# Output and down projections of a fused attention and feed-forward kernel: exact float32 products replaced by three float32r products each

## What is computed

```
h = shift_token(x);  q, k, v = h @ wqkv           # 8 heads of 64, l2norm and rotary on q, k
o = local_attention(q, k, v)                      # windows of 128, each query sees its own and the previous window
x = x + o @ wo                                    # "output product", 512 -> 256
h = layernorm(shift_token(x)) * ln_g + ln_b
a, g = split(h @ w1 + b1)                         # 2 x 682 columns
x = x + (a * gelu(g)) @ w2 + b2                   # "down product", 682 -> 256
```

## Time and profile before

| what | value |
|---|---|
| median of three runs | 1547.39 us |
| the profiled execution, its own time | 1549.65 us |
| span of that execution in the trace | 1547.9 us |
| TensorE (PE) busy | 1471.8 us, 95% |
| DVE, ACT, POOL busy | 895.6, 791.1, 637.7 us |
| mean granted clock of TensorE | 0.98 |
| PE's share of the chain that ended last | 79% |

### The profile page before, as it was taken

One profiled execution on the slowest core, in us unless ns is written; L12 is line 12 of the kernel. 1 busy time (PEld: TensorE's weight loads), 2 busy tenths in 40 slices (PEclk: granted clock), 3 DMA queues, 4 the chain that ended last, 5 costly groups with the idle time before them and its releaser, 6 DMA issues.

```text
span 1547.9 us, 23333 instructions
## 1 busy us (share of the span) xinstructions
PE 1471.8 (95%) x7572; PEld 1020.7 (66%) x7572; DVE 895.6 (58%) x2555; ACT 791.1 (51%) x2073; POOL 637.7 (41%) x424
## 2 busy tenths in 40 slices
PE   3999988999999999999999999999999999999977
PEld 2777766676767676767575766666666666666745
DVE  3677647565656565656565655565655555555635
ACT  1555545464646454645455554646464636464642
POOL 2343326353526253535353534444453535353510
PEclk7999989999999999999999989999999999999998
DMA  6110110000000000000001010000000000000045
GB/s 188 41 54 27 41 64 1 1 1 1 0 0 0 0 0 0 0 0 0 0 1 55 1 55 1 1 0 0 0 0 0 0 0 0 0 0 0 0 141 185
DMA packets 35239, 33.28 MB, mean 21 GB/s; under 512 B 8364, under 2 KB 32896, under 8 KB 35200
## 3 DMA queue, kind: packets, MB, share of 16 engines
q1 hardware_dynamic: 35200, 32.79, 6.6%
HBM read 24.39 MB, written 8.39 MB: 21 GB/s over the span
## 4 chain that ended last, share of the span: by engine, by line
PE 79%; ACT 3%; issue 1%; POOL 1%; DVE 1%; ACTq 0%; POOLq 0%
PE l_psF L1159 9%; PE l_ring L1129 8%; PE l_psP L1129 8%; PE l_psF L1244 7%; PE l_ring L1159 7%; PE l_ring L1227 7%; PE l_ring L1168 6%; PE l_psP L1211 6%; PE l_psS L1168 5%; PE l_psF L1197 4%; PE l_psS L1180 3%; PE l_psS L1197 2%; ACT l_att L875 2%; PE l_psF L1143 2%; PE l_psF L1137 2%
## 5 line engine op out<-in xcount | busy, mean ns | idle before, releaser
L758 POOL TENSOR_TENSOR l_att<-l_att 128x1024 f32<-128x1024 f32 x64 | 153.5, 2398 | 353.5 <-DVE l_att L967 353.5
L796 POOL TENSOR_TENSOR l_att<-l_att,l_rinv 128x1024 f32<-128x1024 f32 x64 | 121.3, 1895 | 84.9 <-DVE l_rinv L1019 84.9
L857 ACT ACTIVATE l_att<-l_psP 128x384 f32<-128x384 f32 (+1 forms) x128 | 70.4, 550 | 164.4 <-PE l_psP L1211 164.4
L1024 DVE COPY l_att<-l_psP 128x384 f32<-128x384 f32 (+1 forms) x128 | 78.8, 615 | 122.1 <-PE l_psP L1211 121.7
L1211 PEld LDWEIGHTS l_psP<-ident,l_att 128*128 128x128 f32 x896 | 100.2, 142 | 50.2 <-issue 45.9
L800 POOL TENSOR_TENSOR l_att<-l_att,l_rinv 128x256 f32<-128x256 f32 x64 | 39.3, 614 | 210.8 <-DVE l_rinv L1019 210.8
L1211 PE MATMUL l_psP<-ident,l_att 128*128 128x128 f32 x896 | 123.8, 279 | 2.1 <-DVE l_att L1024 2.1
L765 POOL TENSOR_TENSOR l_att<-l_att,l_rn 128x1024 f32<-128x1024 f32 x64 | 121.4, 1908 | 0.0
L1244 PE MATMUL l_psF<-l_att,w_wo 128*128 128x512 f32 x256 | 118.5, 606 | 0.0
L875 ACT ACTIVATE l_att<-l_psF,l_nb 128x256 f32<-128x256 f32 x256 | 117.8, 482 | 0.1
L1227 PE MATMUL l_ring<-l_att 128*64 128x256 f32 (+1 forms) x1024 | 111.0, 358 | 4.4 <-issue 2.9
(11 more groups left out here) (171 smaller groups left out, 3695.2 us busy)
## 6 DMA issues: line engine op xcount, KB each, us to landing
a_tables<-in_x SPq DMA_DIRECT2D x8, 512.0 KB, 4.1
scratch_s<-a_o SPq DMA_DIRECT2D x8, 512.0 KB, 3.0
l_att<-in_x SPq DMA_DIRECT2D x8, 512.0 KB, 8.6
l_att<-scratch_s SPq DMA_DIRECT2D x8, 512.0 KB, 9.0
out_dram<-l_att SPq DMA_DIRECT2D x7, 512.0 KB, 7.6
aw_stage<-in_wqkv SPq DMA_DIRECT2D x2, 768.0 KB, 7.3
l_att<-in_wqkv SPq DMA_DIRECT2D x2, 768.0 KB, 5.2
w_w<-in_w SPq DMA_DIRECT2D x2, 640.0 KB
```

What stands on the lines that cost most here:

```text
L758: pool.tensor_tensor(rot[:, t, :], rot[:, t, :], t2[t % 2], ALU.add).then_inc(S["added"], 1)
L796: pool.tensor_tensor(pr, pr, along(inv, 2 * P), ALU.mult).then_inc(S["p_done"], 1)
```

## The change

It touches six things.

1. `output` and `down` use three float32r products for each float32 product: (w_hi, data_hi), (w_hi, data_lo), (w_lo, data_hi). The weights wo and w2 are split once for each layer: high parts on ACT, low parts on DVE.
2. The gated tiles: gelu writes into a gate buffer, DVE's `gated` multiplies in place, ACT's new `u_high` rounds it to U_hi, and DVE's new `u_low` makes U_lo. In merged steps the gate buffers are the four halves of two of the probability buffers (`between_units`), and softmax(0) and softmax(1) wait for the low parts that still read them.
3. The attention result: `o_evac` writes OT_hi, and DVE's new `o_low` makes OT_lo.
4. `mean` and `variance` are one float32 product each: DVE adds the two halves of h (into rstdF), and the two halves of the squares (`sum_squares`), beforehand.
5. The order: down's half c = 0 runs as four tiles before unit 2, then one tile each in units 2 and 4; half c = 1 as tiles 0 to 2, 3 to 4 and 5 in units 7, 8 and 9. add_ffn(0) moves from unit 4 to unit 5. less_mean moves into rotate(0), and ACT's square stands before the second tile's squares.
6. Memory: several buffers share places, and the staging place of wqkv moves. The scratch size for DMA descriptors is set to 4096.

```diff
+    def high_wo(self, act, layer):
+        act.wait_ge(self.S["wo_in"], 16 * (layer + 1))
+        act.activation(self.wo_hi[:, :, :], self.wo_raw[:, :, :], ACT.Copy).then_inc(self.S["wo_hi"], 1)
+
+    def low_wo(self, dve, layer):
+        dve.wait_ge(self.S["wo_hi"], layer + 1)
+        dve.tensor_tensor(self.wo_lo[:, :, :], self.wo_raw[:, :, :], self.wo_hi[:, :, :].bitcast(F32), ALU.subtract).then_inc(self.S["wo_lo"], 1)
...
+    def high_w2(self, act, layer):
+        act.wait_ge(self.S["w2_in"], 32 * (layer + 1))
+        for r, k in self.w2_parts(layer):
+            last = act.activation(self.w2_hi[r, k, :], self.w2_raw[r, k, :], ACT.Copy)
+        last.then_inc(self.S["w2_hi"], 1)
+
+    def low_w2(self, dve, layer):
+        dve.wait_ge(self.S["w2_hi"], layer + 1)
+        for r, k in self.w2_parts(layer):
+            last = dve.tensor_tensor(self.w2_lo[r, k, :], self.w2_raw[r, k, :], self.w2_hi[r, k, :].bitcast(F32), ALU.subtract)
...
                         W.high_w1(act, 0, stage1, k)
+                    W.high_wo(act, 0)
+                    W.high_w2(act, 0)
...
+                    W.low_wo(dve, 0)
+                    W.low_w2(dve, 0)
...
-                if j >= 2:
-                    ge(act, S["u_done"], HT * u + j - 1)
+                if j >= 4:
+                    ge(act, S["u_lo"], HT * u + j - 3)
...
+            def u_high(i, j, attn):
+                rows = P if j < HFULL else HREM
+                ge(act, S["u_done"], HT * (i - 1) + j + 1)
+                act.activation(U_hi[0:rows, j, :], gate_of(j, attn)[0:rows, :], ACT.Copy).then_inc(S["u_hi"], 1)
...
-                act.activation(OT[:, pair, :], ring[pair % 2][:, :], ACT.Copy).then_inc(S["o_sb"], 1)
-
-            def softmax(i, u):
+                act.activation(OT_hi[:, pair, :], ring[pair % 2][:, :], ACT.Copy).then_inc(S["o_hi"], 1)
+
+            def softmax(i, u, ffn):
                 ge(act, S["pT_ps"], UNITS * i + u - 2)
+                if ffn and u < 2:
+                    ge(act, S["u_lo"], HT * (i - 1) + 2 * u + 4)
...
                 if attn:
                     evacuate(i, 0)
-                    evacuate(i, 1, square if ffn else None)
+                    if ffn:
+                        square()
+                    evacuate(i, 1)
...
                 for j in range(HT):
                     if ffn:
-                        gelu(i, j, lf)
+                        gelu(i, j, lf, attn)
+                    if ffn and j:
+                        u_high(i, j - 1, attn)
                     if attn and j < TT:
                         q_evac(i, j)
                     if attn and j == 1:
                         high((i + 1) % B, i + 2)
+                    if turn and j == TT:
+                        W.high_wo(act, 1)
                 if attn:
                     act.preload_act_table_set(NLE)
+                    if ffn:
+                        u_high(i, HT - 1, attn)
...
+                    if turn:
+                        W.high_w2(act, 1)
...
+            def u_low(i, j, attn):
+                rows = P if j < HFULL else HREM
+                ge(dve, S["u_hi"], HT * (i - 1) + j + 1)
+                dve.tensor_tensor(U_lo[0:rows, j, :], gate_of(j, attn)[0:rows, :], U_hi[0:rows, j, :].bitcast(F32), ALU.subtract).then_inc(S["u_lo"], 1)
...
+            def o_low(i, pair):
+                ge(dve, S["o_hi"], PAIRS * i + pair + 1)
+                dve.tensor_tensor(OT_lo[:, pair, :], ring[pair % 2][:, :], OT_hi[:, pair, :].bitcast(F32), ALU.subtract).then_inc(S["o_lo"], 1)
...
+                def sum_squares():
+                    ge(dve, S["sqF_done"], i)
+                    dve.tensor_tensor(sqF[:, 0, :], sqF[:, 0, :], sqF[:, 1, :], ALU.add).then_inc(S["sq_sum"], 1)
...
                 if attn:
-                    rotate(i, 0, la)
+                    rotate(i, 0, la, less_mean if ffn else None)
                 if attn and ffn:
-                    less_mean()
+                    sum_squares()
...
                     combine(2)
                     combine(3)
-                    gated(i, 0, lf)
+                    gated(i, 0, lf, attn)
                     combine(4)
...
                 for j in range(HT):
                     if ffn:
-                        gated(i, j, lf)
+                        gated(i, j, lf, attn)
                     if attn and j < TT:
                         k_evac(i, j)
+                    if ffn and j:
+                        u_low(i, j - 1, attn)
+                if ffn:
+                    u_low(i, HT - 1, attn)
                 if turn:
 
                     ge(dve, S["u_done"], HT * i)
                     dve.memset(stage1[:, :, 2 * HFULL * P:], 0.0).then_inc(WS["w1pad"], 1)
+                    W.low_wo(dve, 1)
                 if attn:
                     for u in range(UNITS + 3):
                         if u < UNITS:
                             least_of(i, u)
                         if 1 <= u <= UNITS:
                             inverse_sum(i, u - 1)
-                        if u == 4 and ffn:
+                        if u == 5 and ffn:
                             add_ffn(i, 0, lf)
                         if u >= 3:
                             p_evac(i, u - 3)
+                        if u in (7, 9):
+                            o_low(i, (u - 7) // 2)
                         if turn and UNITS <= u < UNITS + KD:
                             W.low_w1(dve, 1, stage1, u - UNITS)
+                if attn:
+                    o_low(i, PAIRS - 2)
                 if ffn:
                     add_ffn(i, 1, lf)
+                if attn:
+                    o_low(i, PAIRS - 1)
                 if last:
                     for k in range(KD):
                         W.low_wqkv(dve, 1, stage, k)
+                if turn:
+                    W.low_w2(dve, 1)
                 if attn:
                     ge(dve, S["wo_ps"], i + 1)
                     for k in range(KD):
...
                     ge(dve, S["x_attn"], KD * (i + 1))
-                    dve.tensor_scalar(dF, h_view(xT, i - B * la), 1.0, None, ALU.mult).then_inc(S["h_ready"], 1)
+                    h = h_view(xT, i - B * la)
+                    dve.tensor_tensor(rstdF[:, :].unsqueeze(1), h[:, 0:1, :], h[:, 1:2, :], ALU.add).then_inc(S["h_sum"], 1)
+                    dve.tensor_scalar(dF, h, 1.0, None, ALU.mult).then_inc(S["h_ready"], 1)
...
             def mean(i):
-                ge(pe, S["h_ready"], i)
-                for k in range(KD):
-                    last = pe.matmul(psF[:, 0:N], ones[:, :], dF[:, k], start=(k == 0), stop=(k == KD - 1))
-                last.then_inc(S["mean_ps"], 1)
+                ge(pe, S["h_sum"], i)
+                pe.matmul(psF[:, 0:N], ones[:, :], rstdF[:, :], start=True, stop=True).then_inc(S["mean_ps"], 1)
...
             def variance(i):
-                ge(pe, S["sqF_done"], i)
-                for k in range(KD):
-                    last = pe.matmul(psF[:, N:2 * N], ones[:, :], sqF[:, k, :], start=(k == 0), stop=(k == KD - 1))
-                last.then_inc(S["var_ps"], 1)
+                ge(pe, S["sq_sum"], i)
+                pe.matmul(psF[:, N:2 * N], ones[:, :], sqF[:, 0, :], start=True, stop=True).then_inc(S["var_ps"], 1)
...
-                    if c == 0 and k >= HFULL - 1:
-                        ge(pe, S["u_done"], HT * (i - 1) + k + 1)
-                    last = pe.matmul(down_of[c], w2[:, k, c * P:(c + 1) * P], U[:, k, :], start=(k == 0), stop=(k == HT - 1))
+                    if c == 0:
+                        ge(pe, S["u_lo"], HT * (i - 1) + k + 1)
+                    for m, (w, u) in enumerate(((W.w2_hi, U_hi), (W.w2_hi, U_lo), (W.w2_lo, U_hi))):
+                        last = pe.matmul(down_of[c], w[:, k, c * P:(c + 1) * P], u[:, k, :], start=(k == 0 and m == 0), stop=(k == HT - 1 and m == 2))
...
-                    ge(pe, S["o_sb"], PAIRS * i + pair - 1)
+                    ge(pe, S["o_lo"], PAIRS * i + pair - 1)
...
-                    ge(pe, S["o_sb"], PAIRS * i + a + 1)
+                    ge(pe, S["o_lo"], PAIRS * i + a + 1)
                     for c in range(KD):
-                        last = pe.matmul(psF[:, c * N:(c + 1) * N], wo[:, a, c * P:(c + 1) * P], OT[:, a, :],
-                                         start=(a == 0), stop=(a == PAIRS - 1))
+                        for m, (w, o) in enumerate(((W.wo_hi, OT_hi), (W.wo_hi, OT_lo), (W.wo_lo, OT_hi))):
+                            last = pe.matmul(psF[:, c * N:(c + 1) * N], w[:, a, c * P:(c + 1) * P], o[:, a, :],
+                                             start=(a == 0 and m == 0), stop=(a == PAIRS - 1 and m == 2))
...
-                    down(i, 0, range(0, 3))
+                    down(i, 0, range(0, 4))
                 if attn:
                     for u in range(2, UNITS + 3):
                         if u < UNITS:
                             scores(i, u)
-                        if ffn and 2 <= u <= 4:
```

(11 more changed lines are left out.)

109 lines of the change are left out of this document (67 added, 42 removed).

## The result

The changed kernel takes 1523.69 us (median of 4 runs, 1522.57 to 1525.51), against 1547.97 (4 runs) for the kernel before: a ratio of 0.984, 95% interval [0.983, 0.986]. It is 24 us faster where 45 were forecast, and the time lies 3.7 us above the range of 1480 to 1520. The profiled execution took 1522.57 us, its span 1520.8. In experiments 5 and 6 one execution of four took 1984 and 1982 us at a mean granted clock of 0.65, so their medians here are of the other three.

The account below looks back on a forecast made before the run. PE (TensorE) was taken as the bound, busy 78.50 of 79.24 us in a merged step. Fifteen steps at 3.3 us less (49.5) and +4.9 for single places gave -44.6 us: 1502.8 us against the median, range 1480 to 1520.

Parts of the forecast that it names:

- rival 3: Merged steps: clock falls at the scores(2) hole, some 4 us or more a step, 1563 us in all; chance 0.04.
- Front of a step: Projections to transposes(1): PE 1.7 us earlier, a new wait of 0.6 us at transposes(1), gain 1.1 us a step.
- Middle: hidden(5) to scores(7): least_of(0) 2.3 us late, PE stands 1.7 us at scores(2); net 0.4 us lost a step.
- End of a step: After scores(7): down's second half 1.0 us and output 1.5 us shorter, no new wait; gain 2.6 us a step.
- (a): Before the layers block: low parts of wo and w2 enter DVE's queue, +1.4 us.
- (b): Step 0, attention only: only output gets shorter, -1.5 us.
- (c): Step 7: low_wqkv is queued behind o_low(3) and step 8's projections wait for it, +1.5 us.
- (d): Step 8, the turn: high_wo and low_wo stand before least_of(0), +2.2 us, less 0.6 for output(0) at half clock.
- (e): Step 16: sum_squares stands behind combine(1), which waits for a DMA; after what down gives back, +1.9 us.
- Rival 1: Merged steps: PE's saving arrives nearly whole, 4.3 to 5.5 us a step, 1488 down to 1470 us; chance 0.17.
- Rival 2: Front: POOL holds DVE's sum_squares, gain falls to 1.4 us a step, 1531 us; chance 0.14 with other long waits.
- Rival 4: The float32r products gain nothing, as alternating weights run slower; 1547 + 8 us or so; chance 0.02.

Follow-up runs that it names:

- experiment 5: Changed kernel with one move on DVE: the sixth low part, u_low(5), stands behind least_of(0) instead of ahead of it; 1489.34 us, ratio 0.962.
- exp. 6: Against experiment 5: u_high(5) moved behind softmax(0) on ACT, u_low(5) behind least_of(1) and the first reciprocal on DVE; 1519.04 us, ratio 0.982.
- exp. 1: Changed kernel with 7 unneeded float32r products in each merged step, in PE's standstill before scores(2); 1510.22 us, ratio 0.976.
- exp. 2: Changed kernel with 3 unneeded float32r products in each merged step, in PE's standstill before scores(2); 1511.05 us, ratio 0.976.
- experiment 4: Kernel before the change with two unused 128x1024 multiplications on DVE ahead of least_of(0) in merged steps but the turn; 1582.83 us, ratio 1.022.
- exp. 3: Changed kernel with one unused 128x1024 multiplication on DVE ahead of least_of(0) in merged steps but the turn; 1554.9 us, ratio 1.005.
- Experiment 9: On experiment 5: sum_squares ahead of combine(1) in step 16, one low part of the next projection weights ahead of step 7's last o_low; 1483.59 us.
- experiment 8: On experiment 5: mean and variance again as two float32 products each, without h_sum and sum_squares on DVE; 1509.75 us, ratio 0.976.
- experiments 10: On Experiment 9: in step 8 high_wo on ACT and low_wo on DVE stand behind the last softmax; 1478.04 us, ratio 0.955.
- experiment 7: Changed kernel with down again one float32 product, in its old tile order, without u_high and u_low; 1509.66 us, ratio 0.975.

## Why the prediction was wrong

Most steps of the working held in their mechanism. **What failed is rival 3, the fall of the clock: it stood in the sum at nothing and was given a chance of 4 in 100 for all steps or none.** The prediction set it aside because "a hole of 1.7 us is less than what step 0 had before its fall, and dense products stand on both sides". One example of a fall is no bound from below. The experiments give the other side of it:

| standstill of PE before small products | steps with a fall, of the 14 merged ones but the turn, in one profiled execution each |
| --- | --- |
| 0.2 us (exp. 1), 0.4 us (exp. 5), 1.1 us (exp. 2) | 0 |
| 1.8 us (the changed kernel) | 8 |
| 1.9 us (exp. 4, exp. 6) | 6 and 8 |
| 3.1 us (exp. 3) | 14, four of them about twice as long |

The turn agrees. Its standstills of 2.4, 3.3 and 4.0 us (experiments 1 and 2, the changed kernel) each brought a fall, those of 2.1 us in two runs of four (experiments 5 and 9, not 6 and 8), those of 0.4 and 1.3 us (experiments 10 and 7) none.

A fall costs 1.5 us, not the 4 of the rival: the clock was back some 3 us after it fell, before p_transposes(1). At 8 x 1.5 = 12 us it is most of the miss of 17.5 us between the forecast for the profiled execution (1549.65 - 44.6 = 1505.05) and its 1522.57. The rest by steps:

- **A steady step.** Forecast 75.94 us; the undisturbed one takes 76.17, so 14 x 0.23 = 3.2 us without the turn. Three larger errors partly cancel in it: the front gained 1.64 us (forecast 1.1), the middle lost 0.65 (forecast 0.4), the end gained 2.07 (forecast 2.6). PE's saving was put at 5.5 us a step. PE's busy time says 78.50 - 73.79 = 4.7: norm 1.64 (75.43 in experiment 8 less 73.79 in experiment 5, forecast 1.72), output 78.50 - 75.56 - 1.64 = 1.30 (experiment 7, forecast 1.5) and down 75.56 - 73.79 = 1.77 (experiments 7 and 5, forecast 2.3). Down was mis-sized most, and of its 1.77 only 76.30 - 74.78 = 1.52 shorten a step even in experiment 5. A tile that stands alone between scores costs 0.89 to 0.91 us where it cost 1.05, so it gives 0.15 and not 0.19, and the standstill of 0.4 takes its part.
- **Front of a step.** The new wait of 0.6 us at transposes(1) did not come, though the mechanism was right. In the kernel before, DVE stood just as long for gelu(0) as now:

```profile
635.49 0.75 DVE L981 SCALAR_TENSOR_TENSOR l_ffn<-l_psF,w_b,l_ffn 128x512 f32<-128x512 f32 x1 [2.54 <-ACT l_ffn L849]
```

  gelu(0) stands behind ACT's table load, and that behind ACT's Ln of DVE's last square sum:

```profile
624.37 0.22 ACT L865 ACTIVATE l_lnq<-l_lnq 128x16 f32<-128x16 f32 x1 [2.32 <-DVE l_lnq L1041]
...
624.85 1.28 ACT L894 ACT_TABLE_LOAD   x1
```

  So k_evac(0) starts 627.54 - 622.90 = 4.64 us behind the last square sum, exactly as before. Two small things were wrong. That sum starts at T+20.0, not T+20.4 (T is 602.91 here), so k_evac(0) ends at T+25.3, not T+25.7. And PE starts transposes(1) at 627.93 with four products of q, which don't wait for k_evac(0). The first product of k starts at 628.36, 0.14 us behind the end of k_evac(0). The wait was covered, with almost nothing to spare.
- **Middle.** Late by 2.53 (forecast 2.3), standstill 1.8 (forecast 1.7); scores(7) follows the end of hidden(5) by 18.83 us where it was 668.09 - 649.91 = 18.18, 0.65 later (forecast 0.4). The mechanism was right and its sizes were close. Experiment 5 shows the price of the late least_of: 1.4 us a step.
- **End of a step.** No wait, as forecast, but the gain from scores(7) on was 21.78 - 19.71 = 2.07 us instead of 2.6. Down's second half gave 0.97 (forecast 1.0) and output 1.3 (forecast 1.5), and the last p_transposes, behind the last down tile, take 1.06 us where they took 0.88.
- **Single places.** (a) +0.7 us instead of +1.4. (b) Step 0 gave about nothing instead of -1.5 (63.5 us against 63.65). Its length follows its clock: with the output of the change it takes 62.4 us at a mean clock of 0.96, 63.1 at 0.93, 63.5 at 0.92 and 64.4 at 0.89. With the output of before it takes 63.65 at 0.94 and, in experiment 4, 65.3 at 0.89. At like clock the change gives 0.6 to 0.9 us there, and the rest went to a clock that was low for longer in the profiled execution. (c) Step 7 is 1.1 us longer than an undisturbed one, forecast 1.5. (d) The turn took 87.96 us against 88.87 - 3.3 + 1.6 = 87.17 by the prediction's terms. Here too the clock moves the length: the same turn of the kernel before took 88.87 us at a clock of 0.94 and 85.6 at 0.98 in experiment 4. PE stood 4.0 us before scores(2). (e) Step 16 grew from 56.10 to 59.50, by 3.4 instead of 1.9. variance ran at the low clock (2.07 us for what takes 0.86), which the sum did not have. Experiment 9 gives back 3.9 us there with sum_squares ahead of combine(1). With the falls and the steady steps these places add up to 17.8 us, against the 17.5 that were missed.

**The other rivals.** Rival 1 (saving nearly whole, 1470 to 1488) is wrong for this order of the queues; experiment 5 comes close to it with 1489. Rival 2 did not happen: sum_squares at 610.77 took 0.68 us. POOL's add ended at 610.80, just there. Rival 4 is refuted by the chain: 4.40 us for 18 records.

**Two engines on SBUF.** The prediction priced a two-input add beside POOL at 0.23 us more than alone. u_low(0) is the test. It started at 630.11 and took 2.04 us where it takes 0.68 alone, and POOL on its timeline:

```profile
627.84 3.76 POOL L812 TENSOR_TENSOR l_att<-l_att,l_rn 128x1024 f32<-128x1024 f32 x2
631.57 2.64 POOL L816 TENSOR_TENSOR l_hlo<-xT,l_hhi 128x1024 fp32r<-128x1024 f32 x1
```

The second of the two scales started at 629.70, ahead of u_low(0), and ended at 631.60; u_low(0) ended at 632.15, 0.55 us behind that. So nearly all of its 0.68 us came after POOL's instruction, and POOL's next one was slowed in turn (2.64 us, 2.19 in the mean before). The price was 1.36 us, not 0.23. It cost nothing here, because DVE still stood 0.40 us before gated(2), but some three quarters of the slack that covered it was used. The Trainium skill's page "SBUF — State Buffer", section "SBUF: two separate sides", says that when an instruction of VectorE with two SBUF inputs meets one of GpSimd that reads SBUF, the one that started first keeps the other out until it is over. By that rule u_low(0) waits for the scale, and the trace agrees. The prediction was also wrong to say that all of the new two-input work reads SBUF twice: o_low reads one of its operands from the PSUM ring.

**The number.** The range reached to 1520 for rival 2 and had no place for a fall in part of the steps. With the 12 us of the falls in the sum it would have read 1515, inside the range that was given.

## What to carry to other kernels

Where one engine is the bound and its product gets cheaper, look for the first instruction whose operand makes a round through two other engines, and put it behind whatever the bound engine waits for next: one line moved here was worth more than the whole change. Price a new standstill of PE at its length, and again for the clock: in this kernel nothing up to 1.1 us, 1.5 us in half the cases near 1.8 us, and at least that always at 3.1 us. All of these stood before small products; whether dense ones behind the standstill would have kept the clock up was not tried. When a kernel's repeated stage shows two lengths, compare the granted clock in the same few microseconds of a short and a long one before looking at dependences. And test each part of a large change alone: the down part cost more than it gave.

## What was not expected of the hardware

Near 1.8 us the fall comes in about half of the repetitions of one and the same standstill (steps 1, 3, 4, 6, 9, 10, 12 and 14), with the same instructions around it, and a second execution with another order of queues has it in other steps (2, 4, 5, 7, 10, 11, 13 and 15). Adding 24 us of useless work to TensorE made the kernel 13 us faster. A two-input operation of VectorE that started behind one of GpSimd took three times as long as alone. What decides which of the equal standstills brings a fall was not settled by these runs.
